# A 16-sequence transformer layer on Trainium2: the input's transposes in groups of four token blocks, and a blocked layout that the projections read with a stride

## The chip, the cores and the metric

The kernel runs on one Trainium2 chip (trn2), on all 8 of its NeuronCores. Each core takes 2 of the 16 sequences; the cores share nothing but the inputs. The metric is the device time of the slowest core in microseconds (us). A core has a matmul engine (TensorE, PE in the rows; its weight loads are PEld), a vector engine (VectorE, DVE), an activation engine (ScalarE, ACT), a GpSimd engine (POOL) and a sync engine (SyncE, SP), which here issues every DMA.

## The reference

One layer of a post-norm transformer over x of 16 x 2048 x 1024 in float32. Attention has 16 heads of 64; the feed-forward part has its weights rounded to three levels and its activations to whole numbers.

```python
def attn(x, Wq, Wk, Wv, Wr):
    q = (x @ Wq).reshape(b, s, 16, 64)
    k = (x @ Wk).reshape(b, s, 16, 64)
    v = (x @ Wv).reshape(b, s, 16, 64)
    scores = 0.125 * einsum('bqhd,bkhd->bhqk', q, k) - 50.0 * triu(ones, k=1)
    return einsum('bhqk,bkhd->bqhd', softmax(scores), v).reshape(b, s, 1024) @ Wr

def ffn(x, w_gate, w_up, w_down):
    gate = silu(bitlinear(x, w_gate))
    return bitlinear(gate * bitlinear(x, w_up), w_down)

x = layernorm(x + attn(x, Wq, Wk, Wv, Wr))
x = layernorm(x + ffn(x, w_gate, w_up, w_down))
```

## The kernel before

A core works through its 2 sequences one after the other, with a barrier over all engines between them. A small planner (`Plan`) records every instruction on its engine's list in the order in which the Python code calls for it, with the semaphore values that it waits for; nothing is reordered. So the order on each engine is the order of the code.

A sequence has three parts.

1. *Input.* Four DMAs bring x (2048 tokens x 1024) into `x_tm`, 128 tokens on the partitions and 16 token blocks (`tc`) of 1024 features along the free dimension. VectorE makes two bfloat16 halves of it: `xhi`, the rounded value (one cast over all 16384 columns, L198), and `xlo`, the rest (one scalar_tensor_tensor, L193). Both are transposed by DMA, since the projections need features on the partitions: 16 transposes of `xhi` into `XT_hi` and 16 of `xlo` into `XT_lo`, one of each per token block, hi and lo in turn. One transposes 128 x 1024 values (256 KB). In `XT_hi` and `XT_lo` the 2048 tokens of one chunk `dh` of 128 features stand side by side, chunk after chunk: column `dh * 2048 + token`.
2. *Attention*, in 8 pairs of heads (`attn_pair`). For each pair Wq, Wk and Wv columns come into `wstage`, are split into `apwh` and `apwl`, and are projected (`project`): for each of the four groups of 512 tokens (`qt`, taken two by two) there are 24 matmuls, 8 feature chunks in each of three products (`apwh` with `XT_hi`, `apwh` with `XT_lo`, `apwl` with `XT_hi`). The stationary operand is the 128 x 128 weight block, the moving one is 512 tokens of `XT_hi` or `XT_lo`. Scores, exponentials, the product with V and the normalization follow. In sequence 0 the feed-forward weights are prepared in the gaps, as work for VectorE and the DMA queue (`pw`, `pterf`, `pter`, `pterT`, `pacc` in the rows).
3. *Output projection and first norm* (`wr_ln1`), whose quantized result `xqtm` is transposed by 4 DMAs per sequence into `XqT`, four token blocks each (128 x 4096 values, 1 MB), and then the *feed-forward part* (`ffn`).

What orders the transposes is `dmat` (L146 to 153). A transpose waits for every DMA recorded before it (the `fence` over the 8 DMA semaphores), and leaves its own token as `dma_floor`, on which every later plain DMA waits as well. So transposes run one at a time, each issued after the one before has landed, and the first weight loads of a sequence (`prefetch_w`, recorded behind the transposes) are issued after the last of them. The first matmuls of `project` wait through `t_XT_for` for the last transposes of both kinds, whichever tokens they read.

Of the kernel before, what the change touches and what calls it, by code (L numbers as in the profile page):

```python
# [98 lines left out]
class Builder:  # L99
# [321 lines left out]
    def run_seq(self, s):  # L421
        c = self.c
        S, D, DC = c.S, c.D, c.DC
        with ExitStack() as _es0:
            XT_hi = _es0.enter_context(self.sbg("XT_hi", [128, DC * S], BF16, is_transpose_dest=True)).ap()
            XT_lo = _es0.enter_context(self.sbg("XT_lo", [128, DC * S], BF16, is_transpose_dest=True)).ap()
            with ExitStack() as _es1:
                x_tm = _es1.enter_context(self.sbg("x_tm", [128, c.TC * D], F32, side="right")).ap()
                xhi = _es1.enter_context(self.sbg("xhi", [128, c.TC * D], BF16)).ap()
                xlo = _es1.enter_context(self.sbg("xlo", [128, c.TC * D], BF16)).ap()  # L430
                nx = max(1, c.TC // 4)
                t_x4 = [self.dma(
                    x_tm[:, i * 4 * D:(i + 1) * 4 * D]
                    .rearrange("p (tc d) -> p tc d", tc=4),
                    self.x_in[s][i * 512:(i + 1) * 512, :]
                    .rearrange("(tc p) d -> p tc d", p=128))
                    for i in range(nx)]
                t_hi = self.copy(xhi, x_tm, waits=t_x4)
                t_lo = self.stt(xlo, x_tm, 1.0, xhi, ALU.mult, ALU.subtract,
                                waits=[t_hi])  # L440
                t_Xh_l, t_Xl_l = [], []
                for tc in range(c.TC):
                    t_Xh_l.append(self.dmat(
                        XT_hi.rearrange("p (dh tcc tl) -> p tcc dh tl",
                                        dh=DC, tcc=c.TC)[:, tc],
                        xhi[:, tc * D:(tc + 1) * D], waits=[t_hi]))
                    t_Xl_l.append(self.dmat(
                        XT_lo.rearrange("p (dh tcc tl) -> p tcc dh tl",
                                        dh=DC, tcc=c.TC)[:, tc],
                        xlo[:, tc * D:(tc + 1) * D], waits=[t_lo]))  # L450
            self.t_XT_parts = (t_Xh_l, t_Xl_l)

            wstage = _es0.enter_context(
                self.sbg("wstage", [128, 3 * D], F32)).ap()
            _al0 = lambda *a, **k: _es0.enter_context(self.sbg(*a, **k)).ap()
            nbufs = (_al0("rls", [128, 512], F32),
                     _al0("rlb", [128, 1024], BF16),
                     _al0("osr", [64, 512], F32),
                     _al0("onf", [64, 512], F32),
                     [_al0("ogh0", [64, 512], BF16),  # L460
                      _al0("ogh1", [64, 512], BF16)],
                     [_al0("ogl0", [64, 512], BF16),
                      _al0("ogl1", [64, 512], BF16)])
            self.prefetch_w(0, wstage)
            if s == 0:
                with ExitStack() as _esp:
                    self.prep_alloc(_esp)
                    def _gen():
                        for w in ("g", "u", "d"):
                            yield from self.prep_weight_gen(w)  # L470
                    self.prep_gen = _gen()
                    for pair in range(c.PAIRS):
                        self.attn_pair(s, pair, XT_hi, XT_lo, wstage, nbufs)
                    self.flush_norm()
                    self.pump_prep(10 ** 6)
            else:
                for pair in range(c.PAIRS):
                    self.attn_pair(s, pair, XT_hi, XT_lo, wstage, nbufs)
                self.flush_norm()
        self.barrier()  # L480

        with ExitStack() as _es2:
            XqT = _es2.enter_context(self.sbg("XqT", [128, DC * S], BF16, is_transpose_dest=True)).ap()
            cg_cols = _es2.enter_context(self.sbg("cg_cols", [128, c.TC], F32)).ap()
            cu_cols = _es2.enter_context(self.sbg("cu_cols", [128, c.TC], F32)).ap()
            self.wr_ln1(s, XqT, cg_cols, cu_cols)
            self.barrier()
            self.ffn(s, XqT, cg_cols, cu_cols)
# [20 lines left out]
    def attn_pair(self, s, pair, XT_hi, XT_lo, wstage, nbufs):  # L509
        c = self.c  # L510
        S, D, DC, QT, KC = c.S, c.D, c.DC, c.QT, c.KC
        with ExitStack() as _es:
            al = lambda *a, **k: _es.enter_context(self.sbg(*a, **k)).ap()

            wh = al("apwh", [128, D], BF16)
            wl = al("apwl", [128, D], BF16)
# [10 lines left out]
            def load_split(name):  # L527
# [6 lines left out]
                self.wsplit_toks[name] = [t_h, t_l]  # L534
                return [t_h, t_l]

            def project(t_w, evac):
                toks = []
                grp = [None, None]
                for qp in range((QT + 1) // 2):  # L540
                    js = [j for j in (0, 1) if 2 * qp + j < QT]
                    grp = [None, None]
                    for ph, (wop, xop) in enumerate(((wh, XT_hi), (wh, XT_lo),
                                                     (wl, XT_hi))):
                        for dh in range(DC):
                            last = (ph == 2 and dh == DC - 1)
                            for j in js:
                                qt = 2 * qp + j
                                bk = (2 * (qp % 2) + j) if QT > 2 else j
                                w0 = (t_w + [self.bank_user[bk]]  # L550
                                      + self.t_XT_for(qp)) \
                                    if (ph == 0 and dh == 0) else ()
                                grp[j] = self.mm(
                                    self.bank[bk],
                                    wop[:, dh * 128:(dh + 1) * 128],
                                    xop[:, dh * S + qt * 512:
                                        dh * S + qt * 512 + 512],
                                    ph == 0 and dh == 0, last, waits=w0)
                    for j in js:
                        bk = (2 * (qp % 2) + j) if QT > 2 else j  # L560
                        toks.append(evac(2 * qp + j, bk, grp[j]))
                return toks, [g for g in grp if g is not None]
# [50 lines left out]
            for h in (0, 1):  # L613
# [3 lines left out]
                                waits=[t_qk[-1], self.last_score_tok])  # L617
                t_q1 = self.copy(klp[h][rh, :], qk["q"][0][rh, :],
                                 waits=[t_sh, t_qk[-1]])
                t_q2 = self.dma(klp[h][ro, :], qk["q"][0][rh, :],  # L620
                                waits=[t_sh, t_qk[-1]])
# [23 lines left out]
            for h in (0, 1):  # L645
                hi_q, lo_q = qk["q"]
                for qt in range(QT):
# [8 lines left out]
                    for kc in range(kc_hi):  # L656
# [6 lines left out]
                                      True, False, waits=w0)  # L663
# [607 lines left out]
```

How the kernel before makes its waits and increments, by code:

```python
                def body(eng):  # L77
                    last = {}
                    for emit, waits, inc, tag in plans.ops[eng_name]:
                        for s, v in waits:
                            if last.get(s, -1) >= v:
                                continue
                            eng.wait_ge(plans.sems[s], v)
                            last[s] = v
                        try:
                            instr = emit(eng) if emit is not None else None
                        except Exception:
                            print(f"EMIT FAILED at {tag} on {eng_name}")
                            raise
                        if inc is not None:
                            s, k = inc
                            instr.then_inc(plans.sems[s], k)
```

## Time and profile before

| | us |
|---|---|
| two timed runs | 7136.7 and 7334.0 |
| their median | 7235.35 |
| the profiled execution | 7117.91 |
| its span on the slowest core (core 1) | 7116.4 |
| spans of the 8 cores | 7083.2 to 7116.4 |
| granted TensorE clock of the 8 cores | 0.857 to 0.859 of full speed |

The span goes from the first to the last instruction of a core; what lies around it is 1.5 us. The trace is that of core 1 in the profiled execution. TensorE is busy for 71% of the span, VectorE for 41%, ScalarE for 16%, and the 16 DMA engines for 33% on average. These shares are means over parts with different limits; the prediction reads single stretches.

### The profile page before, as it was taken

What the parts mean: (1) busy time and instruction counts of PE and PEld (TensorE: products, weight loads), DVE (VectorE), ACT (ScalarE), POOL (GpSimd) and SP (SyncE); (2) the same over time, 40 slices, a digit from 0 to 9 for tenths busy, and PEclk for the clock granted to TensorE, in tenths of its full rate; (3) what the DMA queues carried; (4) which work ended last, traced back from release to release, by engine and by line L of the source; (5) the groups of instructions that cost most, each with busy time, mean ns of one, the idle gap of its engine ahead of it and who ended that gap; (6) DMA issues with size and microseconds to landing.
All of it is one profiled execution on the core that took longest, in us unless ns stands there. A gap on an engine that the chain in (4) does not pass through costs nothing.

```text
span 7116.4 us, 56637 instructions; the slowest of 8 cores (7083.2 to 7116.4 us)
## 1 busy us (share of the span) xinstructions
PE 5029.5 (71%) x17938; PEld 1856.7 (26%) x17938; DVE 2896.3 (41%) x4986; ACT 1126.1 (16%) x2132; POOL 0.2 (0%) x4
## 2 busy tenths in 40 slices
PE   0778777876787875575632988888888877567474
PEld 0222222222222332232211223322332233223131
DVE  1545556556554532241312344444444453232231
ACT  0112112112112111010100211222112211011010
POOL 0000000000000000000000000000000000000000
PEclk9888888887888988888876988998899888889797
DMA  4324334334330545445453000000000055545554
GB/s 107 94 74 114 81 101 107 77 92 113 73 72 19 151 124 165 136 142 167 132 158 65 14 16 19 20 9 17 19 19 7 11 138 137 148 131 158 133 151 141
DMA packets 803554, 649.77 MB, mean 91 GB/s; under 512 B 518336, under 2 KB 715200, under 8 KB 803264
## 3 DMA queue, kind: packets, MB, share of 16 engines
q1 hardware_dynamic: 803264, 646.16, 33.3%
q8 instruction: 150, 2.46, 0.1%
q14 instruction: 140, 1.15, 0.1%
HBM read 469.89 MB, written 75.50 MB: 77 GB/s over the span
## 4 chain that ended last, share of the span: by engine, by line
PE 55%; DMA 19%; DVE 14%; issue 5%; ACT 5%; SPq 1%; DVEq 0%; ACTq 0%
PE bank L160 55%; DMA wdsb<-wdT_sc 7%; ACT abuf L171 4%; DVE rls L209 3%; DMA hqT<-hq 3%; DMA XT_lo<-xlo 1%; DMA XT_hi<-xhi 1%; DMA pterT<-pter 1%; SPq L143 1%; DVE pacc L204 1%; DVE vp L198 1%; DMA x_tm<-x 1%; DMA XqT<-xqtm 1%; PE bank L166 1%; DMA pw<-Wu 1%
## 5 line engine op out<-in xcount | busy, mean ns | idle before, releaser
L171 ACT ACTIVATE abuf<-bank,negC 128x512 f32<-128x512 f32 (+3 forms) x1664 | 831.4, 604 | 2936.8 <-DVE bank L188 2119.1
L160 PE MATMUL bank<-abuf,vp 128*65 128x512 f32 x2560 | 1266.4, 654 | 0.0
L160 PE MATMUL bank<-wdsb,hqT 128*128 128x512 bf16 x2048 | 539.1, 414 | 659.0 <-DMA wdsb<-wdT_sc 658.9
L160 PE MATMUL bank<-XT_hi,apwh 128*128 128x512 bf16 x1536 | 424.7, 439 | 582.1 <-DVE apwl L193 405.6
L160 PE MATMUL bank<-klp,khl 128*128 128x512 bf16 x1280 | 506.1, 395 | 404.9 <-ACT abuf L171 381.6
L160 PE MATMUL bank<-wgsb,XqT 128*128 128x512 bf16 x2048 | 496.6, 386 | 243.9 <-DMA wgsb<-wgT_sc 243.1
L209 DVE RECIPROCAL rls<-bank 1x512 f32<-1x512 f32 x128 | 429.5, 3355 | 549.7 <-PE bank L160 548.8
L160 PEld LDWEIGHTS bank<-abuf,vp 128*65 128x65 f32 x2560 | 376.0, 152 | 851.1 <-issue 851.0
L160 PE MATMUL bank<-qlo,khp 128*128 128x512 bf16 x1280 | 510.4, 399 | 0.0
L160 PE MATMUL bank<-wusb,XqT 128*128 128x512 bf16 x2048 | 488.9, 382 | 2.6 <-DMA wusb<-wuT_sc 2.5
L160 PEld LDWEIGHTS bank<-wdsb,hqT 128*128 128x128 bf16 x2048 | 200.0, 104 | 996.7 <-issue 839.4
L188 DVE TENSOR_TENSOR htsb<-bank,gts 128x512 f32<-128x512 f32 x256 | 177.0, 691 | 667.3 <-PE bank L160 613.6
L193 DVE SCALAR_TENSOR_TENSOR z2a<-bank,cdc,z2a 128x512 f32<-128x512 f32 x32 | 22.8, 748 | 891.1 <-PE bank L160 891.1
L160 PEld LDWEIGHTS bank<-XT_hi,apwh 128*128 128x128 bf16 x1536 | 166.4, 110 | 835.3 <-issue 709.5
L160 PEld LDWEIGHTS bank<-klp,khl 128*128 128x128 bf16 x1280 | 125.5, 98 | 891.0 <-issue 864.6
L160 PE MATMUL bank<-XT_hi,apwl 128*128 128x512 bf16 x1536 | 347.2, 379 | 0.0
L160 PE MATMUL bank<-XT_lo,apwh 128*128 128x512 bf16 x1536 | 347.2, 379 | 0.0
L160 PEld LDWEIGHTS bank<-wgsb,XqT 128*128 128x128 bf16 x2048 | 202.2, 99 | 496.5 <-issue 263.6
L171 ACT ACTIVATE gts<-bank,cg_cols 128x512 f32<-128x512 f32 x256 | 176.3, 689 | 685.8 <-PE bank L160 685.8
L160 PEld LDWEIGHTS bank<-wusb,XqT 128*128 128x128 bf16 x2048 | 201.3, 98 | 251.4 <-issue 14.1
L188 DVE TENSOR_TENSOR bank<-bank,mask 128x128 f32<-128x128 f32 x512 | 137.4, 296 | 229.9 <-PE bank L160 224.5
L198 DVE CAST qhi<-bank 128x512 bf16<-128x512 f32 x64 | 43.9, 686 | 384.2 <-PE bank L160 384.2
(90 smaller groups left out, 3450.0 us busy)
## 6 DMA issues: line engine op xcount, KB each, us to landing
wdsb<-wdT_sc SPq DMA_DIRECT2D x256, 512.0 KB, 3.8
wgsb<-wgT_sc SPq DMA_DIRECT2D x64, 1024.0 KB, 6.5
wusb<-wuT_sc SPq DMA_DIRECT2D x64, 1024.0 KB, 9.3
pw<-Wg SPq DMA_DIRECT2D x64, 512.0 KB, 4.7
pw<-Wu SPq DMA_DIRECT2D x64, 512.0 KB, 4.5
pw<-Wd SPq DMA_DIRECT2D x64, 512.0 KB, 4.8
x_tm<-x SPq DMA_DIRECT2D x8, 2048.0 KB, 20.1
xrd<-x SPq DMA_DIRECT2D x32, 512.0 KB, 6.2
```

Of the source, the lines that this page charges most:

```text
L143: e.dma_start(out=o, in_=i), w, (sem, 16))
L160: e.matmul(o, l, r, start=a, stop=b),
L166: e.transpose(o, i, d), waits, ("pe", 1))
L171: e.activation(o, i, f, bias=b, scale=s, accum_out=a),
L188: e.tensor_tensor(o, a, b, p), waits, ("dve", 1))
L193: e.scalar_tensor_tensor(o, a, s, b, p0, p1, accum_out=ac),
L198: lambda e, o=out_ap, i=in_ap: e.tensor_copy(o, i),
L204: e.tensor_reduce(o, i, AX, p, apply_absolute_value=a),
L209: lambda e, o=out_ap, i=in_ap: e.reciprocal(o, i),
```

## The change

The transposes of `xhi` and `xlo` take four token blocks at a time: 4 of each per sequence in place of 16, each over 128 x 4096 values. Their output is laid down block after block, so the layout of `XT_hi` and `XT_lo` is now token block, then feature chunk, then the 128 tokens of the block: column `tc * 1024 + dh * 128 + token in block`. The 512 tokens that a projection matmul reads as moving operand, one run of 512 columns before, are now four runs of 128 columns, 1024 columns (2048 bytes) apart. Nothing else is changed: the number of matmuls, their shapes, the waits of `project` and the order hi, lo, hi, lo stay.

```diff
-                for tc in range(c.TC):
+                for g in range(max(1, c.TC // 4)):
+                    cs = slice(g * 4 * D, min((g + 1) * 4, c.TC) * D)
                     t_Xh_l.append(self.dmat(
-                        XT_hi.rearrange("p (dh tcc tl) -> p tcc dh tl",
-                                        dh=DC, tcc=c.TC)[:, tc],
-                        xhi[:, tc * D:(tc + 1) * D], waits=[t_hi]))
+                        XT_hi[:, cs].rearrange("p (blk tl) -> p blk tl",
+                                               tl=128),
+                        xhi[:, cs], waits=[t_hi]))
                     t_Xl_l.append(self.dmat(
-                        XT_lo.rearrange("p (dh tcc tl) -> p tcc dh tl",
-                                        dh=DC, tcc=c.TC)[:, tc],
-                        xlo[:, tc * D:(tc + 1) * D], waits=[t_lo]))
+                        XT_lo[:, cs].rearrange("p (blk tl) -> p blk tl",
+                                               tl=128),
+                        xlo[:, cs], waits=[t_lo]))
...
+            XhR = XT_hi.rearrange("p (tcc dh tl) -> p tcc dh tl",
+                                  tcc=S // 128, dh=DC)
+            XlR = XT_lo.rearrange("p (tcc dh tl) -> p tcc dh tl",
+                                  tcc=S // 128, dh=DC)
...
-                    for ph, (wop, xop) in enumerate(((wh, XT_hi), (wh, XT_lo),
-                                                     (wl, XT_hi))):
+                    for ph, (wop, xop) in enumerate(((wh, XhR), (wh, XlR),
+                                                     (wl, XhR))):
...
-                                    xop[:, dh * S + qt * 512:
-                                        dh * S + qt * 512 + 512],
+                                    xop[:, 4 * qt:4 * qt + 4, dh],
```

On SyncE's queue, at the start of the program, this stands before (a row is an instruction with its semaphores; the two transposes at the end are the last of 32, and the rows between go on in the same way):

```order
L143 DMA x_tm<-x 128x4x1024 [waits sem_dma5]
L150 DMA_TRANSPOSE XT_hi<-xhi 128x8x128 [waits sem_dve,sem_dma0,sem_dma1,sem_dma2,sem_dma3,sem_dma4,sem_dma5,sem_dma6,sem_dma7]
L150 DMA_TRANSPOSE XT_lo<-xlo 128x8x128 [waits sem_dve,sem_dma6]
L150 DMA_TRANSPOSE XT_hi<-xhi 128x8x128 [waits sem_dma7]
...
L150 DMA_TRANSPOSE XT_hi<-xhi 128x8x128 [waits sem_dma3]
L150 DMA_TRANSPOSE XT_lo<-xlo 128x8x128 [waits sem_dma4]
L143 DMA wstage<-Wq 128x8x128 [waits sem_dma5]
L143 DMA wstage<-Wk 128x8x128
```

and this now, at the same place, with all 8 transposes:

```order
L143 DMA x_tm<-x 128x4x1024 [waits sem_dma5]
L150 DMA_TRANSPOSE XT_hi<-xhi 128x32x128 [waits sem_dve,sem_dma0,sem_dma1,sem_dma2,sem_dma3,sem_dma4,sem_dma5,sem_dma6,sem_dma7]
L150 DMA_TRANSPOSE XT_lo<-xlo 128x32x128 [waits sem_dve,sem_dma6]
L150 DMA_TRANSPOSE XT_hi<-xhi 128x32x128 [waits sem_dma7]
L150 DMA_TRANSPOSE XT_lo<-xlo 128x32x128 [waits sem_dma0]
L150 DMA_TRANSPOSE XT_hi<-xhi 128x32x128 [waits sem_dma1]
L150 DMA_TRANSPOSE XT_lo<-xlo 128x32x128 [waits sem_dma2]
L150 DMA_TRANSPOSE XT_hi<-xhi 128x32x128 [waits sem_dma3]
L150 DMA_TRANSPOSE XT_lo<-xlo 128x32x128 [waits sem_dma4]
L143 DMA wstage<-Wq 128x8x128 [waits sem_dma5]
L143 DMA wstage<-Wk 128x8x128
```

24 transposes are gone, each of the 8 left waits for the one before it as they did, and the load of Wq still waits for the last. The same stands at the start of sequence 1. On TensorE the rows at the start of the first projection are the same before and now (the weight block that each matmul loads is the second name, and the access pattern of the moving operand, which changed, is not in the row):

```order
L160 MATMUL bank<-XT_hi,apwh 128x512 [waits sem_dve,sem_dma4,sem_dma5]
L160 MATMUL bank<-XT_hi,apwh 128x512 x15
L160 MATMUL bank<-XT_lo,apwh 128x512 x16
L160 MATMUL bank<-XT_hi,apwl 128x512 x16
L160 MATMUL bank<-XT_hi,apwh 128x512 x16
L160 MATMUL bank<-XT_lo,apwh 128x512 x16
```

TensorE, VectorE and ScalarE have the same instructions in the same order throughout.

## Rows read from the trace of the kernel before

**Rows 1.** The page: span, and the chain that ended last.
```profile
span 7116.4 us, 56637 instructions; the slowest of 8 cores (7083.2 to 7116.4 us)
...
PE 55%; DMA 19%; DVE 14%; issue 5%; ACT 5%; SPq 1%; DVEq 0%; ACTq 0%
```

**Rows 2.** The chain in order of time, start of sequence 0: start us, us, what.
```profile
33.37 8.71 DVE xhi L198
42.17 17.23 DVE xlo L193
59.53 3.05 DMA XT_lo<-xlo
62.65 3.06 DMA XT_hi<-xhi
...
153.37 3.11 DMA XT_lo<-xlo
156.54 5.40 DMA wstage<-Wq
162.04 0.70 DVE apwh L198
162.83 1.24 DVE apwl L193
164.42 22.36 PE bank L160 x95
```

**Rows 3.** The same view, start of sequence 1.
```profile
3727.33 17.24 DVE xlo L193
3744.70 3.06 DMA XT_lo<-xlo
...
3838.68 3.06 DMA XT_lo<-xlo
```

**Rows 4.** Timeline of SyncE: the first transposes of sequence 0 and of sequence 1.
```profile
42.55 1.33 SPq L150 DMA_TRANSPOSE XT_hi<-xhi  x1
...
3727.50 1.24 SPq L150 DMA_TRANSPOSE XT_hi<-xhi  x1
...
3841.81 0.38 SPq L143 DMA_DIRECT2D wstage<-Wq  x1
```

**Rows 5.** Busy time by stretch: us, busy us (x instructions), clock, DMA share, GB/s.
```profile
core 1: us, PE busy (x) PEld busy (x) DVE busy (x) ACT busy (x) POOL busy (x), PEclk, DMA share, GB/s
59.53:156.54 97.01, 0.00 (x0) 0.00 (x0) 0.00 (x0) 0.00 (x0) 0.00 (x0) 1.00 0.43 84
3744.70:3841.81 97.11, 0.00 (x0) 0.00 (x0) 0.00 (x0) 0.00 (x0) 0.00 (x0) 0.50 0.43 84
```

**Rows 6.** The chain in order of time, the four transposes into XqT.
```profile
2510.99 6.80 DMA XqT<-xqtm
2517.86 6.74 DMA XqT<-xqtm
2524.67 6.73 DMA XqT<-xqtm
2531.47 6.74 DMA XqT<-xqtm
```

**Rows 7.** The tile XqT: its transposes, ns to issue one (min/median/max).
```profile
L150 SPq DMA_TRANSPOSE XqT<-xqtm x8: 4870/5016/5087, 2511.0 to 5947.4; - x8
```

**Rows 8.** TensorE's groups by form, xcount | busy us, mean ns | idle before, releasers.
```profile
L160 PE MATMUL bank<-XT_hi,apwh 128*128 128x512 bf16 x1536 | 424.7, 439 | 582.1 <-DVE apwl L193 405.6 <-DMA wstage<-Wv 176.6
L160 PE MATMUL bank<-XT_hi,apwl 128*128 128x512 bf16 x1536 | 347.2, 379 | 0.0
L160 PE MATMUL bank<-XT_lo,apwh 128*128 128x512 bf16 x1536 | 347.2, 379 | 0.0
```

**Rows 9.** Timeline of TensorE: the first projection, and a run of float32 matmuls.
```profile
164.42 5.30 PE L160 MATMUL bank<-XT_hi,apwh 128*128 128x512 bf16 x16 [164.42 <-DVE apwl L193]
169.56 3.62 PE L160 MATMUL bank<-XT_lo,apwh 128*128 128x512 bf16 x16
173.01 3.62 PE L160 MATMUL bank<-XT_hi,apwl 128*128 128x512 bf16 x16
176.46 3.62 PE L160 MATMUL bank<-XT_hi,apwh 128*128 128x512 bf16 x16
...
304.38 12.21 PE L160 MATMUL bank<-abuf,vp 128*65 128x512 f32 x24
```

**Rows 10.** VectorE's groups by form: a strided and a single-column memset.
```profile
L214 DVE MEMSET vp<- 128x16 f32 x32 | 1.6, 72 | 1.2
...
L214 DVE MEMSET negC<- 128x1 f32 x2 | 0.1, 59 | 0.0
```

## The prediction, made before the changed kernel was run

> **What bounds the kernel now.** I read the page first. By the chain that ended last, TensorE holds 55% of the span, DMA 19% and VectorE 14% [rows 1]. The page is an average over parts, so I went on to the chain in order of time at the place that the change touches, the start of each sequence. In sequence 0 it goes: VectorE casts x to `xhi` (33.37 to 42.1), computes `xlo` (to 59.4), and then come transposes one behind the other, `XT_lo`, `XT_hi`, `XT_lo` and so on, from 59.53 to 156.5; the load of Wq follows, then two VectorE pieces, and the first matmul starts at 164.42 [rows 2]. Sequence 1 does the same from 3744.70 on [rows 3]. The view by stretch shows what the rest of the core does meanwhile: nothing. In 59.53:156.54 and in 3744.70:3841.81 no compute engine has a single instruction, and the DMA engines are busy for 0.43 of the time at 84 GB/s [rows 5]. So these two stretches, 97.01 and 97.11 us, stand on the path whole, with no cover, and whatever shortens them shortens the kernel. They are 194.1 us, 2.7% of the span, and that is also the most that any change to the transposes behind `xlo` could bring.
>
> Why 97 us? A hop, from the issue of one transpose to the issue of the next, is 3.12 us (62.65 - 59.53), of which the transfer is 3.05 [rows 2]. There are 16 + 16 transposes in a sequence. The first, of `XT_hi`, is issued at 42.55 and at 3727.50 [rows 4], while VectorE still computes `xlo`, and is hidden. The other 31 are not: 97.01 / 31 = 3.13 us each.
>
> **The transposes, the term that decides.** The change leaves 8 transposes in a sequence, of four times the size. The trace has exactly this operation: `XqT` from `xqtm`, 128 x 4096 bfloat16, laid down block after block, also one at a time behind the same fence. Four stand in a row at 2510.99, 2517.86, 2524.67 and 2531.47 [rows 6]; a hop is (2531.47 - 2510.99) / 3 = 6.83 us. Again the first of the 8 is hidden: issued at 42.55 it lands near 42.55 + 6.8 = 49.4, and `xlo` is ready only at 59.4, so 10 us of cover are left. The other 7 cost 7 x 6.83 = 47.8 us. Sequence 0 saves 97.0 - 47.8 = 49.2 us, sequence 1 saves 97.1 - 47.8 = 49.3, together 98.5 us.
>
> The two sizes also say where the gain comes from. Four times the data takes 6.83 instead of 3.13, so by a straight line a hop has a part of (4 x 3.13 - 6.83) / 3 = 1.9 us that doesn't grow with the size and 1.23 us for each 256 KB. The data part stays; 24 fixed parts go in each sequence.
>
> At this term a rule of the Trainium skill is to be weighed. DMA: Bandwidth & Descriptors (section Latency and other measured facts) gives a DMA transpose 261 GB/s where the middle dimension is not contiguous and about 350 to 400 where it is, and the change makes the destination contiguous. An estimate from that page: 1.05 MB at 375 GB/s is 2.8 us, and with the 1.9 above a hop would be 4.7, not 6.83. The rows for XqT, which is contiguous already, show 6.83, some 154 GB/s for the whole hop, and I go by them.
>
> **What is late next.** Nothing takes the place of the transposes that go. The load of Wq is issued after the last of them, before and now (the queue rows of the change), and its 5.40 us, then `apwh` and `apwl`, 2.4 us with the steps between, stand behind them as before [rows 2]. Nothing on TensorE, VectorE or ScalarE is reordered, so all that follows starts about 49 us earlier in sequence 0, 98 us earlier in sequence 1 and after. On SyncE's queue the transposes are followed by loads that TensorE needs anyway; no other DMA stands between them, so nothing is delayed by the longer issue of one, 5.0 us [rows 7] against 1.2. The DMA rotation over 8 semaphores keeps its place, since 24 is a multiple of 8.
>
> TensorE's clock could change what the first matmuls cost. The first 16 of the projection take 169.56 - 164.42 = 5.14 us, the next 16 take 3.45 [rows 9]; the granted clock in the stretch ahead of sequence 1's projection is 0.50, the lower of its two levels (1.2 GHz) [rows 5]. After the change TensorE still stands idle for over 115 us first, so the start at the lower level stays as it is. I put it at nothing, with at most 2 us either way.
>
> **The strided read, the term that the trace does not have.** Each projection matmul now reads its 512 moving columns as four runs of 128. There are 3 x 1536 = 4608 of them [rows 8], and they stand on the path: a projection is 95 or so matmuls in one piece of 22.36 us [rows 2]. At the higher clock level 16 take 173.01 - 169.56 = 3.45 us, 216 ns each [rows 9]. What a matmul pays for three jumps no row shows, so I bound it. Below: nothing, since 512 columns stay 512 columns; a gain is excluded, as no shorter stream is asked for. Above, far off, are the float32 matmuls, which read twice the bytes per column at 12.21 / 24 = 509 ns (whole duration, so a little over) [rows 9]; if the jumps halved the reading rate in the same manner, the 293 ns more would be 4608 x 0.293 = 1350 us. Nearer to the pattern, though on another engine and on the writing side, is VectorE's memset of the ones columns of `vp`: 16 elements, each 65 apart, take 72 ns, and a single column takes 59 [rows 10]. So 15 jumps with their elements cost 13 ns, 0.9 ns a jump; three a matmul would be 2.6 ns, times 4608 is 12 us. I take the value nearest to this row's kind, between 0 and 12, and write down 0, because a run of 128 columns is long against one jump. The Trainium skill bears on it too: SBUF — State Buffer (section Door 1: The DMA port swizzle) says that consecutive reads within a 16-byte line run at full rate and that a new line costs. By this rule the change costs nothing, since runs of 256 bytes fill whole lines and 512 columns touch as many lines as before; no row here tests it for TensorE.
>
> **The sum.** It is made against the profiled execution: 7117.9 - 49.2 - 49.3 = 7019.4, say 7020 us, a gain of 1.4%. The two timed runs are 7136.7 and 7334.0, with a median of 7235 that lies 117 us above the profiled one, and they are 2.8% apart; if the time after is such a median, it could lie near 7235 - 98 = 7137, and the upper end of the range takes that in. About 2% is what a measurement of this kernel can tell from no change.
>
> **The rivals.**
>
> *B: the projections slow down.* If a jump stalls the stream of the moving operand, the gain is paid back at TensorE in all 48 projections. The place where it turns is 98.5 us / 4608 = 21.4 ns a matmul, 7 ns a jump (216 to 237 ns). Beyond it the kernel is slower than before; at 240.6 / 4608 = 52 ns (216 to 268) it is slower by over 2%, 7260 us; at the far bound it is 7019 + 1350 = 8370. For it: no row has a moving operand in pieces, and 4608 matmuls multiply a small price. Against it: 0.9 ns a jump in the nearest row, and TensorE's 216 ns is nearly all the time of its columns (512 at 2.4 GHz are 213), so between two matmuls, which is a jump too, it loses under 3 ns. Chance 0.05, of which 0.03 are beyond 2%.
>
> *C: the transposes get cheaper than XqT's.* What a hop can't undercut by the rows is SyncE's time to issue one, 4.87 us at the least [rows 7]. Then sequence 0 saves 97.0 - 34.1 = 62.9, both save 126, and the time is 6992 us. The Trainium skill's rate for contiguous transposes, above, would lead to about the same. Against it: XqT's hop is 6.83 four times over, in the same form. For a gain over 2%, 142 us, a hop would have to be 3.7 us, below the issue time. Chance 0.06.
>
> *D: the gain does not appear*, because a wait that I don't see takes its place (Wq's load late for another reason, or transposes of `xhi` slower than those of `xqtm`, at (97.0 / 7) = 13.9 us a hop). Time 7118. For it: only that hops of 128 x 4096 were measured at another place. Against it: idle engines on both sides and one chain. Chance 0.04.
>
> **The numbers.** The forecast, 98.5 us saved less 0 to 12 for the stride, has 0.85, and its own range is 7005 to 7045. B has 0.05, C 0.06, D 0.04. The range of 6985 to 7140 takes in C, D, B up to its turning point and the spread of the runs. Faster by over 2% is what the spread of runs could make of the forecast or of C: 0.06. Slower by over 2% is B's far part and a little of its spread: 0.04. Within 2%: 0.90.
>
> **What would show it.** Right: in the profile after, 7 hops of 6.8 us between the end of `xlo` and the load of Wq, stretches of 48 us in place of 97, the first matmul near 115 in place of 164.4, 16 projection matmuls still in 3.45 us, the two groups without cold starts still at 347.2 us, and an end 98 us earlier. Wrong: a hop away from 6.8; groups `XT_lo,apwh` or `XT_hi,apwl` over 350 us or with a mean over 379 ns, which is B; or a longer stretch in a part that the change doesn't touch.

## The result, and the profile after

The change is a small gain, as forecast: against the kernel before, the time falls to a ratio of 0.9856, with a 95% interval of 0.9819 to 0.9894. That is 1.4%, within the 2% that a measurement of this kernel can tell from no change, but the interval excludes 1. The profiled execution took 7041.5 us in place of 7117.9. The median over all 11 timed runs of the kernel after is 7142.5 us (the lowest 7016.8, the highest 7592.2), that of the 10 runs before 7375.8 (7121.4 to 7673.7). These two medians are so far above the profiled executions because in more than half of the runs of either kernel the cores of a die (four of the eight) had a lower granted clock; the ratio leaves those out. With 7142.5 the measured median lies 2.5 us above the upper end of my range, 7140.

Which core is the slowest changes from run to run (core 1 before, core 6 after), so the spans of all cores are the better measure of a few tens of us. Before, they are 7083 to 7116 with a mean of 7100.3; after, 6984 to 7040 with a mean of 7009.2. The difference of the means is 91.1 us; 98.5 were forecast. These are single executions: the four quickest timed runs of the kernel after (7016.8 to 7031.0 us) have mean spans of 6995.7 to 7004.1, so against 7100.3 they give 96 to 105 us.

The page of the kernel after, its span and the shares of the chain, to be read beside [rows 1]:

```profile
span 7040.0 us, 56291 instructions; the slowest of 8 cores (6984.3 to 7040.0 us)
...
PE 56%; DMA 19%; DVE 14%; issue 5%; ACT 5%; SPq 1%; DVEq 0%; ACTq 0%
```

The shares hardly show the change: 91 us are less than 2% of the span. The chain in order of time does. Start of sequence 0 (start us, us, what), to be read beside [rows 2]:

```profile
41.52 17.23 DVE xlo L193
58.88 6.67 DMA XT_lo<-xlo
65.62 6.66 DMA XT_hi<-xhi
72.34 6.66 DMA XT_lo<-xlo
79.06 6.66 DMA XT_hi<-xhi
85.78 6.65 DMA XT_lo<-xlo
92.49 6.66 DMA XT_hi<-xhi
99.21 6.71 DMA XT_lo<-xlo
105.98 5.21 DMA wstage<-Wq
111.28 0.70 DVE apwh L198
112.08 1.24 DVE apwl L193
113.67 23.15 PE bank L160 x95
```

Seven transposes stand behind `xlo`, one behind the other, a hop (from the issue of one to the issue of the next) of 6.72 us each, then the load of Wq and the same two VectorE pieces. Seven hops of 6.72 have taken the place of 31 of 3.13. The stretches by themselves, in both sequences (columns as in [rows 5]):

```profile
58.88:105.98 47.10, 0.00 (x0) 0.00 (x0) 0.00 (x0) 0.00 (x0) 0.00 (x0) 1.00 0.82 156
3725.68:3772.82 47.14, 0.00 (x0) 0.00 (x0) 0.00 (x0) 0.00 (x0) 0.00 (x0) 0.50 0.82 156
```

In place of 97.01 and 97.11 us [rows 5] they are 47.10 and 47.14, the compute engines still have no instruction in them, and the DMA engines are busy for 0.82 of the time where they were for 0.43. The same bytes pass in half the time.

The disputed price of the strided read is settled by TensorE's groups by form, to be read beside [rows 8]:

```profile
L160 PE MATMUL bank<-XT_hi,apwh 128*128 128x512 bf16 x1536 | 426.4, 441 | 478.7 <-DVE apwl L193 478.7
L160 PE MATMUL bank<-XT_hi,apwl 128*128 128x512 bf16 x1536 | 347.2, 379 | 0.0
L160 PE MATMUL bank<-XT_lo,apwh 128*128 128x512 bf16 x1536 | 347.2, 379 | 0.0
```

The two groups that never start cold are at 347.2 us and 379 ns to the last digit, as before. The idle time in front of the first group fell from 582.1 to 478.7 us, and this is the gain as TensorE sees it. The timeline of TensorE at the first projection, to be read beside [rows 9]:

```profile
113.67 6.09 PE L160 MATMUL bank<-XT_hi,apwh 128*128 128x512 bf16 x16 [113.67 <-DVE apwl L193]
119.59 3.62 PE L160 MATMUL bank<-XT_lo,apwh 128*128 128x512 bf16 x16
123.05 3.62 PE L160 MATMUL bank<-XT_hi,apwl 128*128 128x512 bf16 x16
```

Sixteen matmuls still take 123.05 - 119.59 = 3.46 us. The sixteen at the start take 5.92 where they took 5.14. In both kernels the first of them come 0.43 us apart, half the pace of the later ones, and the pace doubles within the sixteen, at a different matmul in each. In sequence 1 the granted clock of such a slow start reads 0.50, its lower level (1.2 GHz); in sequence 0 it reads 1.00 in the idle stretch [rows 5] and in the slow start alike, so there the level is read off the pace alone. The point of the doubling scatters: on core 1 the sixteen take 5.14 before and 5.51 after, on core 6 it is 6.26 and 5.92, and the traces below have 4.8 to 6.4.

**Where the 91 us come from.** I cut every core's trace of both kernels at five marks and took the mean over the 8 cores (first projection matmul; first transpose into `XqT`; last load of x of sequence 1; last projection matmul of `XT_hi` with `apwh`; last transpose into `XqT`):

| stretch, mean over 8 cores, us | before | after |
|---|---|---|
| start to the first projection matmul | 162.9 | 113.4 |
| attention and output projection of sequence 0 | 2347.4 | 2348.8 |
| feed-forward part of sequence 0 | 1182.8 | 1189.8 |
| sequence 1, from the load of x to the last projection matmul of `XT_hi` with `apwh` | 1852.5 | 1800.0 |
| to the last transpose into XqT | 393.8 | 392.7 |
| the rest | 1161.0 | 1164.5 |

The two stretches that hold the transposes gain 49.5 and 52.5 us, 102 together. The feed-forward part of sequence 0 and the end give 7.0 and 3.5 back. They contain nothing that the change touches: with the same code there, other kernels of this study have 1183.5 to 1190.0 and 1161.5 to 1167.2. So this is the scatter of single executions, and it is as large as the gap between 91 and 98.5. Core 6, which sets the profiled time after, has 12 us more than the mean in each of attention and the feed-forward part of sequence 0.

### The profile page after: what moved, and what is told of

It is laid out like the page before. It is cut to its first block, busy times and chain, and to the rows that moved or that the text cites. A ratio compares the mean times of both kernels' runs of the same rounds, so it can differ in the third digit from the quotient of the medians.

```text
span 7040.0 us, 56291 instructions; the slowest of 8 cores (6984.3 to 7040.0 us)
## 1 busy us (share of the span) xinstructions
PE 5019.2 (71%) x17688; PEld 1861.6 (26%) x17938; DVE 2894.9 (41%) x4986; ACT 1122.9 (16%) x2132; POOL 0.2 (0%) x4
## 4 chain that ended last, share of the span: by engine, by line
PE 56%; DMA 19%; DVE 14%; issue 5%; ACT 5%; SPq 1%; DVEq 0%; ACTq 0%
PE bank L160 55%; DMA wdsb<-wdT_sc 7%; ACT abuf L171 4%; DVE rls L209 3%; DMA hqT<-hq 3%; DMA pterT<-pter 1%; SPq L143 1%; DVE pacc L204 1%; DVE vp L198 1%; DMA pw<-Wd 1%; DMA wgsb<-wgT_sc 1%; DMA XqT<-xqtm 1%; DMA XT_lo<-xlo 1%; DMA x_tm<-x 1%; PE bank L166 1%
## 5 line engine op out<-in xcount | busy, mean ns | idle before, releaser
L160 PE MATMUL bank<-XT_hi,apwh 128*128 128x512 bf16 x1536 | 426.4, 441 | 478.7 <-DVE apwl L193 478.7
L160 PE MATMUL bank<-klp,khl 128*128 128x512 bf16 x1184 | 466.6, 394 | 396.1 <-ACT abuf L171 389.8
L160 PE MATMUL bank<-XT_hi,apwl 128*128 128x512 bf16 x1536 | 347.2, 379 | 0.0
L160 PE MATMUL bank<-XT_lo,apwh 128*128 128x512 bf16 x1536 | 347.2, 379 | 0.0
```

The lines of the kernel that those rows point to most:

```text
L160: e.matmul(o, l, r, start=a, stop=b),
```

## Experiments

In the diffs below, "after" is the changed kernel.

### The layout and the stride without the grouping

```diff
-                for g in range(max(1, c.TC // 4)):
-                    cs = slice(g * 4 * D, min((g + 1) * 4, c.TC) * D)
+                for g in range(c.TC // 1):
+                    cs = slice(g * 1 * D, (g + 1) * 1 * D)
```

> The change's layout and strided moving operand, but one token block per transpose as before (32 transposes per sequence). Theory F (the gain of 98 us is 24 waits for landing less per sequence, and neither the layout nor the stride has a price): hops of 3.1 us, a stretch of 97 us between xlo and the load of Wq, the groups XT_hi,apwl and XT_lo,apwh at 347.2 us, no difference from the kernel before (ratio 0.997 to 1.003). Rival L (part of the gain comes from the contiguous destination): hops under 3.0 us and a stretch under 93. Rival B (the strided read costs something that the larger gain covered): 16 projection matmuls over 3.45 us, and a time above the kernel before.

Measured: 7132.5 us in the profiled execution, spans with a mean of 7104.3 (before: 7100.3). There is no ratio with an interval for it; its next quickest run took 7144.4 us, and the two quickest of the kernel before in the same session 7134.6 and 7150.4. The chain, start of sequence 0:

```profile
58.83 3.06 DMA XT_lo<-xlo
61.96 3.08 DMA XT_hi<-xhi
...
156.17 3.91 DMA wstage<-Wq
```

and TensorE's groups:

```profile
L160 PE MATMUL bank<-XT_lo,apwh 128*128 128x512 bf16 x1536 | 347.2, 379 | 0.0
L160 PE MATMUL bank<-XT_hi,apwl 128*128 128x512 bf16 x1536 | 347.2, 379 | 0.0
```

Hops of 3.13 us, a stretch of 97.3, and 347.2 us again. The contiguous destination gives nothing to a transpose of this size, and the strided read costs nothing. The rivals L and B are out. What the layout is for is the grouping: the output of a group in the old layout would need one dimension more (block, chunk, token) than the single run of 128-column blocks that the new one has. No run tried a group in the old layout, so what the contiguous destination is worth to a large transpose is not shown.

### Groups of two, eight and sixteen blocks

The same lines with 2, 8 and 16 in place of 4.

> The kernel after with two token blocks per transpose (16 per sequence). From the two measured hops (3.13 us at one block, 6.72 at four) a straight line gives 1.93 us fixed and 1.20 per block. Theory F: a hop of 4.33 us, 15 of them behind xlo, a stretch of 65 us, about 32 us per sequence less than before and 17 more than after. Rival P (the hop is not a straight line but falls per byte only at four blocks and more): a hop of 5 to 6.2 us, a stretch of 75 to 93.

> The kernel after with eight token blocks per transpose (4 per sequence). Theory F: a hop of 1.93 + 8 x 1.20 = 11.5 us, three behind xlo, a stretch of 34.6 us in place of 47.1 after, 12 to 13 us less per sequence. Rival P: the time of a large transpose grows with its bytes alone (1.68 us per block as at four blocks), a hop of 13.4, a stretch of 40.

> The kernel after with all sixteen token blocks in one transpose (2 per sequence). Theory F: 1.93 + 16 x 1.20 = 21.1 us each; the one of xhi is longer than the 17.2 us of xlo that hide it, so 4 us of it stand behind xlo, and the stretch is 4 + 21 = 25 us, 22 us less than after per sequence, 44 us in all. Rival P: 26.9 us each, a stretch of 37.

The chain of the three kernels, behind `xlo` in sequence 0. Groups of two:

```profile
59.17 4.32 DMA XT_lo<-xlo
...
63.56 4.33 DMA XT_hi<-xhi
```

Groups of eight:

```profile
59.24 11.54 DMA XT_lo<-xlo
70.85 11.55 DMA XT_hi<-xhi
...
94.07 5.13 DMA wstage<-Wq
```

One group of sixteen:

```profile
42.19 21.26 DMA XT_hi<-xhi
...
63.52 21.12 DMA XT_lo<-xlo
...
84.71 5.29 DMA wstage<-Wq
```

| blocks per transpose | hop us | 1.93 + 1.20 x blocks | stretch us | mean span us | profiled execution us |
|---|---|---|---|---|---|
| 1 (layout alone) | 3.13 | 3.13 | 97.3 | 7104.3 | 7132.5 |
| 2 | 4.39 | 4.33 | 65.9 | 7048.6 | 7079.0 |
| 4 (after) | 6.72 | 6.73 | 47.1 | 7009.2 | 7041.5 |
| 8 | 11.61 | 11.5 | 34.8 | 6981.3 | 6997.9 |
| 16 | 21.2 | 21.1 | 25.8 | 6959.0 | 6986.1 |

The stretch goes from the end of `xlo` (58.8 to 59.2) to the load of Wq. The last two columns are of one execution each. A hop is a fixed 1.9 us and 1.20 us for each 256 KB, over sixteen times the size. The rival P (no straight line: the price per byte falls only at four blocks, and from there the time goes with the bytes alone) would have given 5 us or more for two blocks and 13.4 and 26.9 for eight and sixteen, and is out. With sixteen blocks the transpose of `xhi` outlasts its cover, as worked out: `XT_lo` is issued at 63.52, when `XT_hi` has landed, not at 58.9. The mean span is 50 us below that with four blocks, where 44 were expected.

### The moving operand in more pieces

The projections read other columns here, so they compute something else. The pieces have 32 columns (64 apart), then single columns 2 apart, then single columns 16 apart. Everything else is the kernel after. The diff is that of the first; `xop` is `XT_hi` or `XT_lo` itself there, and the others take `w=2` and `w=16` with `0:1`, over as many columns as 512 steps need.

```diff
-                                    xop[:, 4 * qt:4 * qt + 4, dh],
+                                    xop[:, (4 * dh + qt) % 16 * 512:
+                                        (4 * dh + qt) % 16 * 512 + 1024]
+                                    .rearrange("p (n w) -> p n w",
+                                               w=64)[:, :, 0:32],
```

> The kernel after, with the moving operand of each projection matmul in 16 runs of 32 columns, 64 apart, in place of 4 runs of 128 (it reads other tokens and features, so the projections are of other data; all else is left). Theory F (a jump inside the moving operand is free as long as a run fills whole lines): 16 projection matmuls in 3.45 us, 347.2 us for XT_hi,apwl and XT_lo,apwh, no change of time. Rival B (a jump has a small price that three jumps did not show): 15 jumps at 0.9 ns, the figure of VectorE's memset, are 13 ns a matmul, 3.66 us for 16, and 60 us on the whole kernel.

> The same with every column a run of its own, 2 columns (4 bytes) apart: 511 jumps a matmul (other data again). Theory F in its strict form says that jumps as such are free, so still 3.45 us for 16 and 347.2 us for a group. Rival B: at 0.9 ns a jump 460 ns more a matmul, 10.8 us for 16, and a kernel of 9100 us. If only bytes fetched count (twice as many): anything between 3.45 and 6.9.

> The same with single columns 16 apart (32 bytes; other data again), so that every column lies in another 16-byte line. Theory F: jumps that leave a line cost, the four-run layout is free only because its runs are whole lines; then a matmul takes longer here, up to twice (6.9 us for 16) or more, and the kernel is 1000 us slower or more. The strictest form, no access pattern costs TensorE anything: 3.45 us for 16, no change of time.

Runs of 32: the projection's timeline has 3.62 us for a group of 16 in the old places and its groups are at 347.2 us, 379 ns; the mean span is 7015.4, against 7009.2. With single columns 2 apart the two groups are at 361.7 us in place of 347.2, and the mean span is 7056.4, so what I called the strict form (jumps as such are free) misses by 4%:

```profile
121.00 3.76 PE L160 MATMUL bank<-XT_lo,apwh 128*128 128x512 bf16 x16
124.59 3.76 PE L160 MATMUL bank<-XT_hi,apwl 128*128 128x512 bf16 x16
```

Single columns, 16 apart:

```profile
114.91 14.85 PE L160 MATMUL bank<-XT_hi,apwh 128*128 128x512 bf16 x16 [114.91 <-DVE apwl L193]
129.58 14.87 PE L160 MATMUL bank<-XT_lo,apwh 128*128 128x512 bf16 x16
```

| moving operand of 512 columns | us for 16 | ns a matmul |
|---|---|---|
| 1 run of 512 (before) | 3.45 | 216 |
| 4 runs of 128 (after) | 3.46 | 216 |
| 16 runs of 32 | 3.45 | 216 |
| 512 single columns, 4 bytes apart | 3.59 | 224 |
| 512 single columns, 32 bytes apart | 14.7 | 918 |

So neither three nor fifteen jumps can be seen. My bound of 0.9 ns a jump, from VectorE's memset, was an upper bound without meaning for TensorE: at 511 jumps it would have cost 460 ns, and 8 were measured. What does cost is leaving the line with every column: 918 ns, 1.8 ns a column in place of 0.42. The kernel with it takes 10300 us. The rule of the Trainium skill that I cited (SBUF — State Buffer, section Door 1: The DMA port swizzle), that reads are at full rate while they stay in a 16-byte line and that each new line costs, has the right direction here: 8 columns of bfloat16 fill such a line, and the last row of the table touches one line per column. The price does not grow evenly with the lines, though: by that line length 64 lines become 128 in the fourth row for 8 ns, and 512 in the last for 702. Steps of 4 and 8 columns were not run, so where the price sets in, and that it is the line and not the distance between the columns, is not shown.

### The kernel before, with its transposes unchained

The old layout and all 32 transposes, but each waits for its data alone (and for the last user of its own semaphore). The first projection and every later DMA wait for all 32, because the memory of `xhi` and `xlo` is used again.

```diff
+    def dmat_free(self, out_ap, in_ap, waits=()):
+        sem = self.dma_sems[self._dma_rot]
+        self._dma_rot = (self._dma_rot + 1) % self.NDMA
+        return self.p.add("sync", lambda e, o=out_ap, i=in_ap:
+                          e.dma_start_transpose(o, i),
+                          list(waits) + [(sem, self.p.counts[sem])],
+                          (sem, 16))
...
-                    t_Xh_l.append(self.dmat(
+                    t_Xh_l.append(self.dmat_free(
...
+            self.dma_floor = t_Xh_l + t_Xl_l
...
-        return [h[-1], l[-1]]
+        return h + l
```

> The kernel before (old layout, 32 transposes per sequence), but the transposes of xhi and xlo wait only for their data, not for each other; the first projection and all later DMAs wait for all of them. Theory F (a hop's fixed 1.9 us is the wait for the landing of the one before; the rest is the 1.22 us that SyncE takes to issue 256 KB): the 16 of xhi go in 16 x 1.22 = 19.5 us from 42.5 on, 2.3 us past the end of xlo, the 16 of xlo follow in 19.5, and with 1.9 for the last landing the stretch from 59.5 to the load of Wq is 24 us in place of 97, provided xhi's are issued ahead. In the order hi, lo, hi, lo of the code the first lo holds the queue until xlo is there, so 31 issues stand behind it: 31 x 1.22 + 1.9 = 39.7 us, 57 us less per sequence, 115 in all, 7003 us: faster than the change, with the small transposes and the old layout. Rival Q (the fixed part is work of the DMA engines, and waiting is only how it shows): still near 3.1 us each, a stretch of 90 or more, no gain.

Measured: a ratio of 0.9836 to the kernel before (0.975 to 0.9922), 7043.0 us profiled, a mean span of 7016.6. SyncE's timeline (start us, us to issue):

```profile
60.16 1.22 SPq L148 DMA_TRANSPOSE XT_lo<-xlo  x1
61.48 1.25 SPq L148 DMA_TRANSPOSE XT_hi<-xhi  x1
62.83 1.26 SPq L148 DMA_TRANSPOSE XT_lo<-xlo  x1
...
95.69 2.93 SPq L148 DMA_TRANSPOSE XT_lo<-xlo  x1
...
102.72 1.26 SPq L148 DMA_TRANSPOSE XT_lo<-xlo  x1
105.96 0.38 SPq L142 DMA_DIRECT2D wstage<-Wq  x1
```

and the stretch:

```profile
60.16:105.96 45.80, 0.00 (x0) 0.00 (x0) 0.00 (x0) 0.00 (x0) 0.00 (x0) 1.00 0.99 178
```

This is the test of why a hop has a fixed part. Taking away the wait for the landing brings the 31 small transposes from 97.0 to 45.8 us, as little as the change reached with 7 large ones (47.1), in the old layout and with contiguous reads. A hop falls from 3.13 to 1.35 us, by 1.8, so nearly all of the fixed 1.9 is the wait, and the rival Q, work of the DMA engines that remains, is out. The DMA shares say the same: share times stretch, divided by the blocks of 256 KB in it, is 1.35 us with 31 small transposes (0.43 of 97.0 us, the kernel before), 1.38 with 7 large ones (0.82 of 47.1) and 1.46 here. The engines have about the same work in all of them, and what goes is the time in which they have none. The size was not quite mine: a small one occupies the queue for 1.35 us, not 1.22, so the stretch is 45.8 and not 39.7 (one of them even 2.93), and the kernel is as fast as the change, where I had expected it to be faster. The view by stretch shows that the DMA engines are now busy for 0.99 of it. SyncE is nearly full as well (1.26 us of each 1.35), so that the DMA engines set the pace is likely, by their 1.35 us a block, but not shown.

### The kernel after, unchained, in quarters, and with early weights

The first edit is that of the section before, in the kernel after.

> The kernel after (four token blocks per transpose), with the transposes of xhi and xlo waiting only for their data. Theory F: what is left of a hop is SyncE's issue time, 4.8 us, so from the end of xlo 7 x 4.85 + 1.9 = 36 us to the load of Wq, in place of 47.1 in the kernel after, 11 us less per sequence; and less than the 45.8 us of the unchained small ones, since a small one costs 1.35 us of queue (5.4 for four). Rival Q (the large transposes are bound by the DMA engines' own work): near 47 us as before.

Measured: the stretch from the end of `xlo` (59.90) to the load of Wq (97.14) is 37.24 us. The execution took 7326.6 us, at the lower clock named with the result, so only this stretch is read from it, in which no compute engine works.

```profile
59.90:97.14 37.24, 0.00 (x0) 0.00 (x0) 0.00 (x0) 0.00 (x0) 0.00 (x0) 1.00 1.04 197
```

Ten us less than after, as expected (36 against 47), and now at a DMA share of 1.04 (by the view's count it passes 1 here). A hop is 5.1 us, of which the issue takes 5.0, and the DMA engines have no idle time left: 1.04 x 37.24 us over 28 blocks is again 1.38 us a block. I see nothing more to take from the transposes as they are; what is left is to start them sooner.

```diff
-                t_hi = self.copy(xhi, x_tm, waits=t_x4)
-                t_lo = self.stt(xlo, x_tm, 1.0, xhi, ALU.mult, ALU.subtract,
-                                waits=[t_hi])
+                t_his, t_los = [], []
+                for i in range(nx):
+                    xs = slice(i * 4 * D, (i + 1) * 4 * D)
+                    t_his.append(self.copy(xhi[:, xs], x_tm[:, xs],
+                                           waits=[t_x4[i]]))
+                    t_los.append(self.stt(xlo[:, xs], x_tm[:, xs], 1.0,
+                                          xhi[:, xs], ALU.mult, ALU.subtract,
+                                          waits=[t_his[-1]]))
```

> As e9_after_unchained, and xhi and xlo are computed in four quarters, each as soon as its quarter of x has landed, with the transposes of each quarter behind it. Theory F (the start of a sequence is a chain of load, cast, split, transposes, of which now only the longest part should stay): transposes from about 15 us on, 8 x 4.9 us, the last landing near 57 to 62 in place of 105.9 in the kernel after, 45 us less per sequence, 90 in all, about 6930 us. Rival R (loads of x and transposes share the DMA engines, which are busy for 0.67 of the time while x loads): the last landing only at 75 or later, half the gain.

Measured: the load of Wq is issued at 72.2 us (105.98 after), between the two expectations and nearer to that of R. The timeline of SyncE says why:

```profile
2.10 5.77 SPq L142 DMA_DIRECT2D x_tm<-x  x4
15.24 19.40 SPq L148 DMA_TRANSPOSE XT_hi<-xhi  x1
34.81 4.81 SPq L148 DMA_TRANSPOSE XT_lo<-xlo  x1
```

The first transpose is issued at 15.24, as planned, but its issue takes 19.40 us in place of 5, until the loads of x are in (34 us). The other seven follow at 5.1 us. So the rival R holds in the main: a transpose issued behind 8 MB of loads on the same queue is not issued to its end before these have landed. In sequence 1 its issue takes 15.06. The view by stretch has the DMA engines without a gap while it stands there:

```profile
15.00:34.60 19.60, 0.00 (x0) 0.00 (x0) 18.78 (x7) 0.00 (x0) 0.00 (x0) 1.00 1.05 298
```

The 0.67 in my expectation was the mean over 0 to 42 us, which takes in 9 us after the loads; while x loads (3 to 33 us of the kernel before) the share is 0.92, so there was little to fill. Whether it is the queue or the DMA engines that hold the transpose is not separated by this run. There is no ratio for this kernel. Its quickest run has 6978.2 us and a mean span of 6936.7, 72.5 less than after (90 by theory F, half of it by R); the profiled execution took 7248.8, and only the input stretches are read from it.

> As e10_pipeline, with the first Wq, Wk and Wv loads issued before the transposes (wstage lies beside x_tm). Theory F: the 5.2 us of the load of Wq leave the path, the first matmul 2.3 us behind the last landing; 5 us less per sequence than e10, 10 in all. Rival R: the 1.5 MB of weights delay x and the transposes by as much, no difference from e10.

The edit issues `prefetch_w(0, wstage)` ahead of the transposes, with `wstage` beside `x_tm`, and lets the first `apwh` wait for all transposes. Measured: a ratio of 0.9771 to the kernel before (0.9702 to 0.984, so whether it is over 2% stays open), 6970.3 us profiled, mean span 6936.8, against 6936.7 in the quickest run above. The first projection matmul starts at 81.30, where it started at 80.69 in the run above, and the mean spans are the same: nothing gained, so R and not F. The loads of Wq and Wk now hold the queue behind those of x, for 7.79 and 12.74 us, and the first transpose is issued at 33.60.

> As e11_pipeline_wq, with the fence taken from the other transposes too (XqT, hqT and pterT wait for their data, their buffer and the last user of their semaphore). Theory F: XqT's four take 4 x 4.9 + 1.9 = 21.5 us in place of 27 (11 us for both sequences), each of the 16 pairs into hqT loses 1.9 us of its 13.5 and the wait for plain loads in flight, 30 us or more, so some 40 us less than e11 and about 6880 us. Rival S (these transposes stand behind work that hides them): under 10 us less than e11.

The edit puts `dmat_free` in place of `dmat` for `XqT`, `hqT` and `pterT` too. Measured: 0.9662 of the kernel before (0.9586 to 0.9737), 6876.2 us profiled, mean span 6845.2. This is 91.5 us less than the kernel above, twice the 40 of theory F; the rival S (under 10) is out. Cut at the same marks, attention of sequence 0 gives 23.8 us (2346.1 to 2322.3), the feed-forward part of sequence 0 34.3 (1184.6 to 1150.3), the last part 27.0 (1166.0 to 1139.0), and the stretch to the last transpose into XqT 6.7 (390.9 to 384.2). SyncE's timeline in the first feed-forward block of sequence 0, first with the fence (the kernel above):

```profile
2595.35 11.86 SPq L157 DMA_TRANSPOSE hqT<-hq  x2
2608.99 0.81 SPq L142 DMA_DIRECT2D wdsb<-wdT_sc  x2
2614.43 11.81 SPq L157 DMA_TRANSPOSE hqT<-hq  x2
2628.08 39.60 SPq L142 DMA_DIRECT2D wdsb<-wdT_sc  x14
```

and without it:

```profile
2557.65 10.77 SPq L148 DMA_TRANSPOSE hqT<-hq  x2
2568.52 1.00 SPq L142 DMA_DIRECT2D wdsb<-wdT_sc  x2
2569.68 12.24 SPq L148 DMA_TRANSPOSE hqT<-hq  x2
2582.07 40.26 SPq L142 DMA_DIRECT2D wdsb<-wdT_sc  x14
```

With the fence the stretch from the first `hqT` transpose to the run of loads behind the second pair is 32.7 us, without it 24.4. I had counted 1.9 us a pair for the landing. What I had left out is the other side of the fence: the second pair waited for the two loads of `wdsb` in flight (2608.99 to 2614.43), and each load after a pair waited for the pair to land. That was the first block. In the other three of the sequence the two pairs stand apart, each in front of its own 14 loads, and the second one behind two loads. Taken together, the way from the first pair to its loads and the way from those two loads to the second pair's loads get shorter by 8.9, 10.0 and 10.0 us (core 1 of both kernels). With 8.3 in the first block that is 37 us, where the feed-forward part, the transposes into XqT included, gave 34.3; a few us come back in its other parts. The 23.8 us in attention of sequence 0 stood in no term of mine, though I took the fence off `pterT` as well: its 96 transposes are there, and VectorE's waits for them fall from 86.0 to 33.9 us (core 1).

## Why the prediction was right, and where it was wrong

- *The transposes stand on the path whole, without cover.* Right. Both stretches, 97.0 and 97.1 us, turned into 47.1, and all of it reached the first matmul (162.9 to 113.4 on the mean of the cores).
- *The hop of XqT is the hop of the new transposes, 6.83 us.* Right: 6.81 on core 1, the core on which 6.83 was read, and 6.72 on core 6, where seven hops are 47.1 us, not 47.8.
- *A hop has a fixed 1.9 us and 1.23 per 256 KB.* Right from 1 to 16 blocks (1.93 and 1.20), and the unchained kernel shows that nearly all of the fixed part (1.8 of 1.9) is the wait for the landing. The Trainium skill's figure for contiguous transposes (DMA: Bandwidth & Descriptors, section Latency and other measured facts), by which a hop would have been 4.7 us, did not hold: 6.72, and the layout alone changed a hop by nothing (3.13). Even unchained, a megabyte took 5.1 us, 205 GB/s.
- *The strided read costs 0 to 12 us.* Right, with 0. The far end of the bound, 1350 us, has a counterpart in the runs (3200 us with columns 32 bytes apart), but not for runs of 128 columns.
- *Nothing takes the place of what goes; the clock at the start stays as it is.* Right: Wq's load, `apwh` and `apwl` follow as before, the sixteen matmuls of the slow start take 5.92 us (core 6) in place of 5.14 (core 1), and 5.51 on core 1, within the 2 us allowed. The prediction gave the 0.50 of sequence 1 as the clock of this start; the row of sequence 0, where 5.14 was read, says 1.00, and only the pace shows the lower level there.
- *The sum, 98.5 us, 7020 us.* The profiled execution has 7041.5, 76 us below 7117.9, but on another core: core 6, whose attention and feed-forward part of sequence 0 ran 12 us long each. On the mean of the cores it is 91.1, in the two stretches concerned 102, and 96 to 105 by the four quickest timed runs. The ratio 0.9856 is what 7020 to 7118 says, 0.9862.
- *The range, 6985 to 7140.* Wrong, and this is the step that failed: "if the time after is such a median, it could lie near 7235 - 98 = 7137, and the upper end of the range takes that in". I took the spread of two runs, 7136.7 and 7334.0, for the spread to be covered and put the end 3 us above the one point that it gave. Ten runs of the kernel before go from 7121 to 7674, with a median of 7376; eleven after from 7017 to 7592, with 7142.5. So the term that was too small is the spread: 117 us above the forecast of 7020, where the median came out 122.5 above it, and 254 above the quickest run for the kernel before; a range for such a median had to reach to about 7275. That the miss is only 2.5 us is luck: 7142.5 is the sixth of eleven runs, the fifth is 7059.9 and the seventh 7354.8. The mechanism and its size are not touched by that.
- *Rivals.* B (projections slow down): nothing, 347.2 us in both. C (cheaper transposes): chained, a hop stayed at 6.72 to 6.81; unchained it fell to 5.1, near the 4.87 that C had named. D (no gain): did not come.

## What to carry to other kernels

When a stretch of the trace has DMA engines busy for less than half the time and every compute engine idle, look at what each DMA waits for: a chain in which each is issued after the landing of the one before pays a fixed part every time (1.9 us here), and it goes away by larger transfers or by dropping the wait, with the same result (47.1 and 45.8 us); both together gave 37.2. A fence that a helper puts on every call is worth the same look at all its callers; taking it off the other transposes, whose true dependences were written out already, gave another 91.5 us here, as much as the change itself. A moving operand of 512 columns could be read in pieces of 128 and of 32 columns (64 bytes) at no cost; every second column cost 4%, every sixteenth 4 times the time.

## What the runs showed of the hardware that I had not expected

- A matmul of 512 moving columns takes 216 ns in one run, in runs of 128 and in runs of 32 columns, 224 ns with every second column, and 918 ns with every sixteenth: it is not the number of jumps that is paid for, since the last two have the same number.
- A DMA transpose issued while 8 MB of loads are in flight on the same queue holds SyncE for 19.4 and 15.1 us in place of 5, until about when the loads have landed; an earlier issue of it gained only part of what the plan said, and 1.5 MB of weights issued ahead took back what they saved.
- Unchained transposes keep the 16 DMA engines busy for 0.99 (256 KB each, 178 GB/s) to 1.04 of the time (1 MB each, 197 GB/s); chained ones of 256 KB for 0.43 at 84 GB/s.
